# A decoder layer on one core: cross-attention with turned scores, per 512 tokens

## The chip, the cores and the metric

The kernel runs on one core of a Trainium2 chip. Engines: TensorE (PE), VectorE (DVE), ScalarE (ACT), GpSimd (POOL) and SyncE (SP), which only issues DMAs here. The metric is the device time of one execution in microseconds, median of 3 runs.

## The reference

One pre-norm decoder layer on x [2, 1024, 512] and a context ctx [2, 2048, 512], float32:

```
x = x + attn(layernorm(x))          # 16 heads of 32, q and k normed to length 1, band |j-i| <= 16, even distances
x = x + xattn(layernorm(x), ctx)    # one head of 512:
      q = xn @ Wq + bq;  k = ctx @ Wk + bk;  v = ctx @ Wv + bv
      out = softmax(q @ k.T) @ v
x = x + ffn(x)                      # silu(x @ wg.T) * (x @ wu.T) @ wd.T, hidden 1536, int weights / 127
```

Since softmax rows sum to one, the kernel computes cross-attention as softmax(q' ctx^T) ctx Wv + bv with q' = (xn Wq + bq) Wk^T: keys and values are never built.

## The kernel before

The work is a straight list of instructions for each engine; semaphores order them. Nearly all products are float32 in three parts: each operand is split into a high part (rounded to fp32r, by ACT) and a low part (the rest, by DVE), and `three` (line 173) issues high x high, high x low, low x high.

**Self-attention.** Tokens are in NS = 4 sequences of 512. A sequence has 16 slots (`UN`), one head group and token tile each; in a slot PE does scores of the next slot, some work of the neighbouring sequences (norm transposes, projections, output and query projections of the sequence before), and `weighted`. POOL masks the exps, normalises q and k (`scale_units`, ahead of `heads`) and scales outputs. PSUM has 8 banks: `score` (4) and `work` (4). The work banks are a ring: `ring_uses` (line 69) lists every use in order, `take` waits until the use four before is freed. Ahead of the slots come the weights: `part_hi` (ACT) and `part_lo` (DVE) split one part after the other, among them the query and key weights of cross-attention and the output weights (part `WO`, in slot 12 of the first sequence). `turned` splits a normalised, transposed x tile, which the first projections need. `bias_row(("ob",), ...)` makes the output bias from the value bias and the output weights with 12 matmuls, in slot 14 of the first sequence, behind `heads`. Query projections (`project_query`, key "z") give q' in xs and go to DRAM (`qp_scratch`).

**Cross-attention** (`cross_programs`, line 1272) goes over 16 tiles of 128 queries. The turned context `ct_h`/`ct_l` and the context `cn` of one batch lie whole in SBUF in both parts; pieces of 256 context positions come through a staging ring. For a tile g, interleaved with tile g + 1's scores:

- `pe_scores`: 4 banks of [128 queries, 512 context positions], 12 matmuls each with q as the stationary operand
- DVE takes the row maxima from PSUM (`dve_maxima`, `dve_shifts`); ACT computes the exps with row sums (`act_exps`)
- `pe_pt`: 16 transposes turn the exps to [context, queries] (line 1669); ACT and DVE split them (lines 1474, 1549)
- 48 matmuls with 16 context blocks sum [128 queries, 512] in `work[:, 2]`; ACT scales by 1/sum
- `turn`: 4 transposes (line 1679), split, `project`: 12 matmuls with Wv; DVE adds x1 + bv; SP stores x2

Tiles 0 and 1 overlap the end of the last self-attention sequence; the last tile overlaps the transposes of the feed-forward part.

**Feed-forward** (`ffn_programs`): two halves of 1024 tokens, 12 iterations (`NIT`), each with 14 products (a 7-product scheme for gate and up) and, one iteration later, 8 down products. `pe_turn` makes seven turned combinations of the tokens; six of the first half are made during the last cross-attention tile, the seventh in iteration 0. POOL makes token combinations (`pool_tokens`) and weight sums (`pool_weights`).

Of the kernel before, what the change touches and what calls it, by code (L numbers as in the profile page):

```python
# [20 lines left out]
P = 128  # L21
# [31 lines left out]
NSTAGE = 4  # L53
NEARLY = 11
FIRST = 11
# [7 lines left out]
def value_parts(s, n):  # L63

    first = 7 if s == NS - 1 else 4
    return (n - first,) if first <= n < first + ST else ()


def ring_uses():
# [7 lines left out]
    for s in range(NS):  # L77
        more = s + 1 < NS
        for n in range(UN):
            t = n % ST  # L80
            if n == 6:
                yield from (("kt", s, 2), ("qt", s, 2))
# [25 lines left out]
            if not s and n == 14:  # L108
                yield ("ob",)
# [5 lines left out]
    yield from (("o", s, 0), ("o", s, 1), ("o", s, 2), ("y", s, 0), ("o", s, 3), ("y", s, 1), ("pt", 0), ("y", s, 2),  # L115
                ("pt", 1), ("y", s, 3), ("pt", 2))
    yield from (("z", s, m) for m in range(DK))
    yield ("pt", 3)


class Ring:


    def __init__(self, sem, work):
        self.work, self.order = work, list(ring_uses())
        self.nth = {key: n for n, key in enumerate(self.order)}
        self.filled, self.act_freed, self.dve_freed, self.pt_freed = (
            sem(n) for n in ("filled", "act_freed", "dve_freed", "ptl_done"))
        kind = {"v": self.act_freed, "z": self.act_freed, "pt": self.pt_freed}
        self.freed_by = [kind.get(key[0], self.dve_freed) for key in self.order]  # L130
        self.taken = []
# [4 lines left out]
    def wait_filled(self, eng, key):  # L136
        eng.wait_ge(self.filled, sum(k[0] not in ("len", "pt") for k in self.order[:self.nth[key] + 1]))

    def wait_freed(self, eng, key):
        n = self.nth[key]  # L140
        eng.wait_ge(self.freed_by[n], sum(f is self.freed_by[n] for f in self.freed_by[:n + 1]))

# [37 lines left out]
def decoder_layer(nc, x, ctx_n, ctx_t, wqkv_t, qkv_b, wo_t, out_b, wq_t, bq, wk_t, bk, wv, bv,  # L180
# [3 lines left out]
    qp_dram = nc.dram_tensor("qp_scratch", [NT, P, D], F32, kind="Internal").ap()  # L184
    with ExitStack() as ctx:
# [14 lines left out]
        small = [sb(ctx, f"x_{n}", [P, w]) for n, w in (("mx", 4), ("negm", 2), ("shift", 2), ("sums", 4), ("rinv", 2))]  # L200
        at = nc.sbuf_base + -nc.sbuf_base % 32
        links = {n: sem(n) for n in ("exp_done", "pv_done", "o_copied", "x1_stored", "qp_stored", "cb_done")}
        ffn = ffn_programs(nc, Plan(nc, at), sem, score, work, ident, mhalf, wait_pad,
                           wg_t, wu_t, wd_t, x2_dram, out)
        cross = cross_programs(nc, Plan(nc, at), sem, score, work, ident, q_const, small, ring, links,
# [5 lines left out]
def attention_phase(nc, ctx, plan, sem, score, ident, mhalf, wait_pad, q_const, work, ring, links,  # L211
# [158 lines left out]
    qp_v = qp_dram.rearrange("(s t) p n -> s p t n", t=ST)  # L370

    with nc.Block() as block:
        @block.sync
        def _(sp):
# [10 lines left out]
            def store_q(s):  # L385
                wait_freed(sp, ("z", s, DK - 1))
                sp.dma_start(qp_v[s], xs[:]).then_inc(qp_stored, 16)
# [23 lines left out]
            for s in range(NS):  # L411
# [7 lines left out]
                if s == NS - 1:  # L419
# [3 lines left out]
                    cross.load_piece(sp, 0)  # L423
                    cross.load_piece(sp, 1)
                    sp.wait_ge(pv_done, s * UN + UN // 2)
                    cross.load_piece(sp, 2)
                    cross.load_q(sp, 1)
                    for n in range(3, 8):
                        cross.load_piece(sp, n)
# [5 lines left out]
            cross.load_q(sp, 2)  # L435
            for n in range(8, 12):
                cross.load_piece(sp, n)
            store(NS - 1)
            for n in range(12, 16):
                cross.load_piece(sp, n)  # L440
# [121 lines left out]
        def _(act):  # L562
# [81 lines left out]
            def query(s, m):  # L644
                key = ("z", s, m)
                wait_filled(act, key)
                if m == 0:
                    act.wait_ge(x1_stored, 16 * s + 16)
                A.activation(xs[:, :, P * m:P * m + P], bank(key).rearrange("p (t c) -> p t c", t=ST),
                             ACT.Identity, bias=bqp[:, m:m + 1]).then_inc(act_freed, 1)  # L650
# [15 lines left out]
            squares(0, 0, 1)  # L666
# [1831 lines left out]
```

## Time and profile before

| | us |
|---|---|
| median of 3 runs | 1216.77 (1216.16 to 1216.86) |
| profiled execution | 1214.97 |
| its span | 1212.8 |
| PE busy | 1178.3 (97%) |
| DVE / ACT / POOL busy | 746.7 / 494.9 / 418.8 |

Busy times of PE come from modelled ends: matmuls overlap, so the distance of their starts is their cost, not their duration. "Idle before" names who released a waiting engine. The granted clock is in shares of 2.4 GHz.

### The profile page before, as it was taken

To read this page: it belongs to the slowest core of one execution; us is meant where nothing else is said; L and a number is where in the kernel's file an instruction comes from. 1 tells how busy PE (TensorE), PEld (TensorE's weight loads), DVE (VectorE), ACT (ScalarE), POOL (GpSimd) and SP (SyncE) were. 2 spreads that over 40 slices of the span, in tenths; PEclk is the share of its full clock that TensorE was granted. 3 is DMA by queue.
4 is the path that set the end of the run, shared out by engine and by line. 5 is a ranking of instruction groups with operands and counts; after the bars stand their busy time and mean duration, and the time that the engine had idled before them with its cause. 6 is when DMAs were issued, how large, how long until landed. Compare 5 with 4: busy or idle time off the path is not lost.

```text
span 1212.8 us, 17589 instructions
## 1 busy us (share of the span) xinstructions
PE 1178.3 (97%) x6672; PEld 956.6 (79%) x6672; DVE 746.7 (62%) x1268; ACT 494.9 (41%) x854; POOL 418.8 (35%) x382
## 2 busy tenths in 40 slices
PE   6999999999999999999999999999999998999998
PEld 4877777777767888888778888877888887888886
DVE  6667675684686642333563422346899877788875
ACT  5354454454364532222542222236444344444431
POOL 1255765764764010000000100042545742444431
PEclk9999999999999999999999999999999999999999
DMA  8010110201046440000442010021511111511101
GB/s 286 10 36 9 37 62 1 79 36 37 35 140 200 150 154 27 27 26 26 152 127 96 27 35 26 17 79 54 198 53 53 52 53 52 174 53 53 53 18 70
DMA packets 50188, 87.03 MB, mean 72 GB/s; under 512 B 4544, under 2 KB 16832, under 8 KB 50112
## 3 DMA queue, kind: packets, MB, share of 16 engines
q1 hardware_dynamic: 50112, 86.00, 21.5%
q8 instruction: 50, 0.82, 0.3%
q14 instruction: 26, 0.21, 0.1%
HBM read 69.21 MB, written 16.78 MB: 71 GB/s over the span
## 4 chain that ended last, share of the span: by engine, by line
PE 83%; DVE 6%; ACT 4%; POOL 4%; issue 3%; DMA 0%; ACTq 0%; POOLq 0%; DVEq 0%
PE work L175 15%; PE work L177 14%; PE work L176 14%; PE score L177 5%; PE score L175 5%; PE score L176 5%; PE score L2370 4%; PE score L2372 3%; PE score L2371 3%; PE score L1125 2%; PE work L2370 2%; PE work L2372 2%; PE work L2371 2%; PE work L1669 2%; PE score L1139 1%
## 5 line engine op out<-in xcount | busy, mean ns | idle before, releaser
L1549 DVE TENSOR_TENSOR pt_l<-work,pt_h 128x512 fp32r<-128x512 f32 x64 | 44.0, 690 | 168.8 <-ACT pt_h L1474 168.8
L1447 POOL TENSOR_TENSOR xr<-xr,bv_row 128x512 f32<-128x512 f32 x16 | 22.0, 1374 | 333.1 <-DMA xr<-x_scratch 333.1
L2036 POOL TENSOR_TENSOR hid<-fg,hid 128x512 fp32r<-128x512 f32 x48 | 84.8, 1787 | 105.2 <-ACT hid L2100 105.2
L497 POOL TENSOR_TENSOR probs<-probs,band 128x544 f32<-128x544 f32 (+1 forms) x64 | 89.5, 1399 | 78.2 <-ACT probs L628 77.9
L1474 ACT CAST pt_h<-work 128x512 fp32r<-128x512 f32 x64 | 37.3, 587 | 173.1 <-PE work L1669 173.0
L175 PE MATMUL score<-ct_h,x_q_h 128*128 128x512 f32 x256 | 102.8, 401 | 1.6 <-DVE ct_l L1543 1.0
L175 PE MATMUL work<-cn,pt_h 128*128 128x512 f32 x256 | 101.8, 398 | 0.0
L177 PE MATMUL score<-ct_h,x_q_l 128*128 128x512 f32 x256 | 100.1, 391 | 0.0
L177 PE MATMUL work<-cn,pt_l 128*128 128x512 f32 x256 | 99.9, 390 | 0.0
L175 PE MATMUL work<-wqkv_h,xt_h 128*128 128x512 f32 (+1 forms) x256 | 94.9, 371 | 5.2 <-DVE xt_l L804 5.2
L176 PE MATMUL score<-ct_l,x_q_h 128*128 128x512 f32 x256 | 99.9, 390 | 0.0
L176 PE MATMUL work<-cn,pt_h 128*128 128x512 f32 x256 | 99.7, 389 | 0.0
L2248 DVE SCALAR_TENSOR_TENSOR fx<-work,fx 128x512 f32<-128x512 f32 x96 | 65.6, 685 | 40.3 <-PE work L177 40.2
L2370 PE MATMUL score<-fxt,w_hl 128*128 128x512 f32 x222 | 87.1, 392 | 2.2 <-DVE fxt L2196 2.1
L176 PE MATMUL work<-wqkv_l,xt_h 128*128 128x512 f32 (+1 forms) x256 | 88.6, 346 | 0.0
L177 PE MATMUL work<-wqkv_h,xt_l 128*128 128x512 f32 (+1 forms) x256 | 88.1, 344 | 0.0
L2372 PE MATMUL score<-fxt,w_hl 128*128 128x512 f32 x222 | 86.5, 390 | 0.0
L2371 PE MATMUL score<-fxt,w_hl 128*128 128x512 f32 x222 | 86.4, 389 | 0.0
L175 PE MATMUL work<-wd_hl,hid 128*128 128x512 f32 x176 | 68.7, 390 | 0.6 <-DVE fx L2248 0.6
L176 PE MATMUL work<-wd_hl,hid 128*128 128x512 f32 x176 | 68.5, 389 | 0.0
L177 PE MATMUL work<-wd_hl,hid 128*128 128x512 f32 x176 | 68.5, 389 | 0.0
L2100 ACT CAST hid<-fg 128x512 fp32r<-128x512 f32 x48 | 29.7, 621 | 86.8 <-DVE fg L2233 52.0
(243 smaller groups left out, 3025.5 us busy)
## 6 DMA issues: line engine op xcount, KB each, us to landing
x_stage<-in_ctx_t SPq DMA_DIRECT2D x16, 512.0 KB, 4.4
x_stage<-in_ctx_n SPq DMA_DIRECT2D x16, 512.0 KB, 4.8
w_stage<-in_wg_t SPq DMA_DIRECT2D x12, 512.0 KB, 3.7
w_stage<-in_wu_t SPq DMA_DIRECT2D x12, 512.0 KB, 3.7
wd_raw<-in_wd_t SPq DMA_DIRECT2D x12, 512.0 KB, 3.6
x_in<-in_x SPq DMA_DIRECT2D x16, 256.0 KB, 2.7
xs<-in_x SPq DMA_DIRECT2D x4, 1024.0 KB, 5.6
x_scratch<-xs SPq DMA_DIRECT2D x4, 1024.0 KB, 4.4
```

The source lines that it names most:

```text
L175: pe.matmul(out, hi_s, hi_m, start=first, stop=False)
L176: pe.matmul(out, hi_s, lo_m, start=False, stop=False)
L177: return pe.matmul(out, lo_s, hi_m, start=False, stop=last)
L497: PL.tensor_tensor(probs[:, n % 2, :, 0:w], probs[:, n % 2, :, 0:w], band[:, c0:c0 + w].unsqueeze(1).to_broadcast([P, HPG, w]), ALU.mult). ...
L1474: nc.scalar.copy(pt_h[:, 4 * c:4 * c + 4, :], src.rearrange("p (k q) -> p k q", q=P)).then_inc(pth_done, 1)
L1549: V.tensor_tensor(pt_l[:, 4 * c:4 * c + 4, :], src.rearrange("p (k q) -> p k q", q=P), pt_h[:, 4 * c:4 * c + 4, :].bitcast(F32), ALU.subtr ...
L2036: PL.tensor_tensor(hid[:, q, 1, :], g[:, q, :], hid[:, q, 0, :].bitcast(F32), ALU.subtract).then_inc(hidl_done, 1)
L2100: A.copy(hid[:, q, 0, :], g[:, q, :]).then_inc(hidh_done, 1)
L2248: V.scalar_tensor_tensor(xs[:, t, :], work[:, 2 + n % 2, :], WSCALE, xs[:, t, :], ALU.mult, ALU.add)\
L2370: PE.matmul(bank(key), w_h, x_h, start=first, stop=False, skip_group_check=True)
L2371: PE.matmul(bank(key), w_h, x_l, start=False, stop=False, skip_group_check=True)
L2372: last = PE.matmul(bank(key), w_l, x_h, start=False, stop=k == 1, skip_group_check=True)
```

## The change

Cross-attention is written anew, the feed-forward part gets other SBUF places and another start, and the first sequence is reordered.

**Scores turned.** The stationary operand is a block of 128 context positions, the moving one 512 queries of a sequence. j counts 64 slots = 4 sequences x 16 context blocks; a slot is one block of scores (12 matmuls, 18 slots ahead, `LEAD`) and one block of the context product (12 matmuls into 4 banks, result [512 channels in 4 blocks, 512 queries]):

```
+    def pe_scores(pe, j):
...
+            last = three(PE, out, ct_h[:, n % 2, k, c], ct_l[:, n % 2, k, c], q_h[g % 2][:, k, :], q_l[g % 2][:, k, :],
                          k == 0, k == DK - 1)
+    def pe_weighted(pe, j):
...
+            last = three(PE, score[:, d, :], cn_h[:, m % 2, j % 2, c], cn_l[:, m % 2, j % 2, c],
+                         pt_h[:, j % 2, :], pt_l[:, j % 2, :], i == 0, i == CK - 1)
     def pe_program(pe):
+        for j in range(NSL):
+            if j + LEAD < NSL:
+                pe_scores(pe, j + LEAD)
+            if j and not i:
+                pe_sums(pe, g - 1)
+            if i == CK - 2 and g + 1 < NS:
+                pe_maxima(pe, g + 1)
+            if i == CK - 1 and g + 1 < NS:
+                pe_shift(pe, g + 1)
+            if j in RESULT_AT:
+                pe_project(pe, RESULT_AT[j])
+            pe_weighted(pe, j)
```

`pe_pt`, `turn` and the copy scaled by 1/sum are gone. Scores are now copied by ACT to a ring of 20 blocks in SBUF:

```
+    def act_scores(act, j):
+        A.copy(s_at(j), s_bank(j)).then_inc(sc_copied, 1)
+    def dve_maxima(dve, j):
+            V.tensor_tensor(mx[:], mx[:], s_at(j), ALU.max).then_inc(mx_done, 1)
+    def dve_sub(dve, j):
+        V.tensor_tensor(s_at(j), s_at(j), shifts[j // CK % 2][:], ALU.add).then_inc(sub_done, 1)
+    def act_probs(act, j):
...
+        A.activation(pr[:, j % 2, :], s_at(j), ACT.Exp).then_inc(e_done, 1)
+        act.wait_ge(e_done, j + 1)
+        if j >= 2:
+            act.wait_ge(block_done, j - 1)
+        A.copy(pt_h[:, j % 2, :], pr[:, j % 2, :]).then_inc(pth_done, 1)
+    def dve_probs(dve, j):
+        V.tensor_tensor(pt_l[:, j % 2, :], pr[:, j % 2, :], pt_h[:, j % 2, :].bitcast(F32), ALU.subtract)
+    def pool_sum(pool, j):
+            nc.gpsimd.tensor_tensor(acc[:], acc[:], pr[:, j % 2, :], ALU.add).then_inc(acc_done, 1)
```

Once a sequence: `pe_maxima` transposes the running maxima (4), `dve_shift` reduces them, forms the shift per query and copies it wide (`spread`), `pe_shift` multiplies it by the identity (4 float32 matmuls of 128 columns) so that it stands along the free dimension, `act_shift` copies it; `pe_sums` sums the running sum over partitions (4 matmuls of one column). At a sequence's end `act_out`/`dve_out` split the four banks and `pe_project` (12 matmuls, four times, in slots 1 to 4 of the next sequence) multiplies by Wv; 1/sum is applied in `dve_result`. Context and turned context are no longer kept: each piece of 256 positions is loaded and split again for every sequence, two buffers each (ct in even slots, cn mostly in odd ones, in slots 46 to 60 in even ones). The order on ACT and DVE in a slot is: piece, exp and cast (ACT) or add and low part (DVE) for slot j + 1, then copy or maximum of block j + 18.

**Hand-overs.** Blocks 0 to 3 of the scores stand in slots 12 to 15 of the last self-attention sequence, 4 to 17 behind it between the output and query projections:

```
+    yield from (("c", 4), ("c", 5), ("c", 6), ("o", s, 0), ("o", s, 1), ("c", 7), ("o", s, 2), ("y", s, 0), ("c", 8),
+                ("o", s, 3), ("y", s, 1), ("c", 9), ("y", s, 2), ("c", 10), ("c", 11), ("y", s, 3))
+    yield from (("c", j) for j in range(12, CK))
+    yield from (("z", s, 0), ("mt",), ("z", s, 1), ("mb",), ("z", s, 2), ("z", s, 3))
+    yield from (("c", j) for j in range(CK, LEAD))
```

Feed-forward statistics, norms, weight parts and token combinations are spread over slots 28 to 50; five turned combinations stand in slots 52, 54, 57, 60 and 61, two in iteration 0, together with the last sequence's four projections and results.

**First sequence.** ACT, and likewise DVE: turned tiles ahead of weight parts, the query weights' part last:

```
             part_hi(0)
+            turned("x", 0, 0, xt_h, x_hi)
             part_hi(1)
-            turned("x", 0, 0, xt_h, x_hi)
             part_hi(2)
+            turned("x", 0, 1, xt_h, x_hi)
             part_hi(3)
             norm1(0, 2)
-            turned("x", 0, 1, xt_h, x_hi)
             norm1(0, 3)
+            turned("x", 0, 2, xt_h, x_hi)
             part_hi(KEYS)
+            squares(0, 0, 0)
+            turned("x", 0, 3, xt_h, x_hi)
+            squares(0, 0, 1)
             part_hi(WQ)
-            squares(0, 0, 0)
-            turned("x", 0, 2, xt_h, x_hi)
-            squares(0, 0, 1)
-            turned("x", 0, 3, xt_h, x_hi)
```

The output weights are split in slot 3 (ACT) and 4 (DVE) instead of 12, and the bias row moves ahead of `heads` in slot 6:

```
                     if n == 6:
+                        if not s:
+                            pe.wait_ge(set_lo, WO + 1)
+                            bias_row(("ob",), 1, wo_h, wo_l)
                         heads(s, 2)
...
-                    if not s and n == 14:
-                        pe.wait_ge(set_lo, WO + 1)
-                        bias_row(("ob",), 1, wo_h, wo_l)
```

## Rows read from the trace of the kernel before

**Rows 1.** Page, busy time and chain: engine, us, share, instructions; shares of the span

```profile
PE 1178.3 (97%) x6672; PEld 956.6 (79%) x6672; DVE 746.7 (62%) x1268; ACT 494.9 (41%) x854; POOL 418.8 (35%) x382
...
PE 83%; DVE 6%; ACT 4%; POOL 4%; issue 3%; DMA 0%; ACTq 0%; POOLq 0%; DVEq 0%
```

**Rows 2.** Busy time in stretches: PE, weight loads, DVE, ACT, POOL, granted clock, DMA

```profile
0.00:26.00 26.00, 14.11 (x53) 10.86 (x54) 15.79 (x35) 12.78 (x17) 5.57 (x24) 1.00 0.92 323
350.00:400.00 50.00, 47.81 (x284) 36.84 (x282) 36.84 (x61) 24.88 (x42) 23.65 (x23) 0.97 0.49 162
400.00:840.00 440.00, 436.88 (x2103) 361.73 (x2102) 180.05 (x325) 148.41 (x286) 42.84 (x34) 1.00 0.21 67
```

**Rows 3.** Order of time on PE in cross-attention: start us, us, what

```profile
543.39 0.60 PE L1679 MATMUL work<-ident,x_o 128*128 128x128 f32 x4
...
563.18 0.39 PE L175 MATMUL work<-cn,pt_h 128*128 128x512 f32 x1
...
566.58 0.60 PE L1669 MATMUL work<-ident,x_pr 128*128 128x128 f32 x4
566.94 0.48 PE L175 MATMUL score<-ct_h,x_q_h 128*128 128x512 f32 x1
...
570.21 0.60 PE L1679 MATMUL work<-ident,x_o 128*128 128x128 f32 x4
```

**Rows 4.** Groups of instructions of PE: busy us, mean ns, idle before

```profile
L1669 PE MATMUL work<-ident,x_pr 128*128 128x128 f32 x256 | 38.1, 272 | 1.3 <-DVE pt_l L1549 1.3
L1094 PE MATMUL work<-cols,wk_raw 128*128 128x1 f32 x32 | 3.7, 251 | 0.0
```

**Rows 5.** Waits of PE, 838 to 860: us in total, times, longest

```profile
PE work L2370 <- DVE xr L1579: 0.8, 1, 0.8
```

**Rows 6.** Groups of instructions of ACT, DVE and POOL

```profile
L637 ACT COPY o_sc<-score 128x512 f32<-128x512 f32 x16 | 9.6, 597 | 0.0
L1482 ACT ACTIVATE x_pr<-score,x_shift 128x512 f32<-128x512 f32 x64 | 43.1, 687 | 36.4 <-DVE x_shift L1564 36.4
L1474 ACT CAST pt_h<-work 128x512 fp32r<-128x512 f32 x64 | 37.3, 587 | 173.1 <-PE work L1669 173.0
L1468 ACT CAST cn<-x_stage 128x1024 fp32r<-128x1024 f32 x16 | 15.9, 1056 | 0.0
L1549 DVE TENSOR_TENSOR pt_l<-work,pt_h 128x512 fp32r<-128x512 f32 x64 | 44.0, 690 | 168.8 <-ACT pt_h L1474 168.8
L1543 DVE TENSOR_TENSOR cn<-x_stage,cn 128x1024 fp32r<-128x1024 f32 x16 | 20.2, 1288 | 3.1 <-ACT cn L1468 3.0
L2008 POOL TENSOR_TENSOR tn<-fxn 128x1024 f32<-128x1024 f32 x2 | 4.8, 2396 | 5.8 <-DVE fxn L2184 5.8
```

**Rows 7.** Durations: minimum, median, maximum in ns, first and last start

```profile
L2191 DVE TENSOR_TENSOR w_hl<-wsum,w_hl x24: 1208/1225/2316, 820.9 to 1171.9; 128x1024 fp32r<-128x1024 f32 x24
L1447 POOL TENSOR_TENSOR xr<-xr,bv_row x16: 1281/1292/2333, 426.0 to 799.7; 128x512 f32<-128x512 f32 x16
```

**Rows 8.** Order of time at the start: start us, us, what, idle before

```profile
10.76 0.79 PE L175 MATMUL work<-wqkv_h,xt_h 128*128 128x512 f32 x1 [2.07 <-DVE xt_l L804]
20.46 0.47 PE L175 MATMUL work<-wqkv_h,xt_h 128*128 128x512 f32 x1 [0.83 <-DVE xt_l L804]
25.72 0.66 PE L175 MATMUL work<-wqkv_h,xt_h 128*128 128x512 f32 x1 [2.28 <-DVE xt_l L804]
27.02 0.63 PE L175 MATMUL work<-wqkv_h,xt_h 128*128 128x512 f32 x1
16.69 1.91 ACT L568 CAST wq_h<-wq_raw 128x2048 fp32r<-128x2048 f32 x1
20.23 2.28 DVE L815 TENSOR_TENSOR wq_l<-wq_raw,wq_h 128x2048 fp32r<-128x2048 f32 x1
```

**Rows 9.** Order of time in the first sequence, slots 3 and 6

```profile
75.38 0.80 ACT L579 ACTIVATE xn<-x_in,nb,rstd 128x512 f32<-128x512 f32 x1
83.35 1.09 PE L1078 MATMUL work<-ident,qk 128*128 128x128 f32 x8 [0.96 <-POOL qk L491]
```

More of the change, by code:

```diff
@@ L422, in _ @@
                     wait_filled(sp, ("qt", s, 3))
[L423 to L429, printed above, removed]
+                    for n in range(5):
+                        cross.load_ct(sp, n)
                 if s:
@@ L1461, in act_query @@
-    def act_query(act, g, par):
-        act.wait_ge(q_landed, g * 16 + 16)
-        nc.scalar.copy(q_h[:, par, :], q_raw[:]).then_inc(q_hi, 1)
-    def act_split(act, n):
-        act.wait_ge(staged[slot(n)], 16 * sum(slot(m) == slot(n) for m in range(n + 1)))
-        src, hi, _ = split_views(n)
-        nc.scalar.copy(hi, src).then_inc(split_hi, 1)
-    def act_pt(act, g, c):
-        act.wait_ge(pt_ready, g * 4 + c + 1)
-        src = ring.bank(("pt", c)) if starts(g) else work[:, c % 2, :]
-        nc.scalar.copy(pt_h[:, 4 * c:4 * c + 4, :], src.rearrange("p (k q) -> p k q", q=P)).then_inc(pth_done, 1)
@@ L1476, in act_exps @@
-    def act_exps(act, g, par):
-        act.wait_ge(shift_done, g + 1)
-        if not starts(g):
-            act.wait_ge(pt_ready, g * 4)
-            act.wait_ge(sum_done, g)
-        for c in range(SB):
-            nc.scalar.activation(pr[:, 512 * c:512 * c + 512], score[:, c, :], ACT.Exp,
-                                 bias=shift[:, par:par + 1], accum_out=sums[:, c:c + 1]).then_inc(e_done, 1)
-    def act_finish(act, g):
-        act.wait_ge(tr_ready, g + 1)
-        nc.scalar.copy(ot_h[:], work[:, 3, :]).then_inc(oth_done, 1)
@@ new lines, in pe_shift, with pe_sums @@
+    def pe_shift(pe, g):
+        out = ring.take(pe, ("mb",)) if not g else work[:, 3, :]
+        pe.wait_ge(spread_done, g + 1)
+        for t in range(ST):
+            last = PE.matmul(out[:, P * t:P * t + P], spread[:, t, :], ident[:], start=True, stop=True)
+        last.then_inc(mb_ready, 1)
+    def pe_sums(pe, g):
+        pe.wait_ge(acc_done, (CK - 1) * (g + 1))
+        if not g:
+            pe.wait_ge(one_done, 1)
+        if g + 1 < NS:
+            pe.wait_ge(mb_copied, g + 2)
+        else:
+            pe.wait_ge(rinv_done, g)
+        for t in range(ST):
+            last = PE.matmul(work[:, 3, t:t + 1], acc[:, P * t:P * t + P], one[:], start=True, stop=True)
+        last.then_inc(rs_ready, 1)
@@ new lines, in pe_project @@
+    def pe_project(pe, n):
+        g, t = n // ST, n % ST
+        pe.wait_ge(otl_done, DK * g + DK)
+        if not n:
+            pe.wait_ge(wv_lo, 2)
+            ring.wait_last(pe, 2)
+        elif n <= (NS - 1) * ST:
+            pe.wait_ge(x2_done, n)
+        elif t == 1:
+            pe.wait_ge(rinv_done, NS)
+        else:
+            pe.wait_ge(x2_done, n - 1)
+        c = slice(P * t, P * t + P)
+        for d in range(DK):
+            last = three(PE, y_bank(n), ot_h[:, d, c], ot_l[:, d, c], wv_h[:, d, :], wv_l[:, d, :],
+                         d == 0, d == DK - 1)
+        last.then_inc(y_ready, 1)
@@ L1881, in ffn_programs @@
     uses = [key for key in events if key[0] == "x" or (key[0] == "p" and key[3] != 2)]
-    nth_use = {key: n for n, key in enumerate(uses)}
-    banks = [score[:, i, :] for i in range(4)] + [work[:, i, :] for i in range(2)]
+    banks = [work[:, i, :] for i in range(2)] + [score[:, i, :] for i in range(4)]
+    bank_of, last_in, use_ahead, n_ring = {}, {}, {}, 0
+    for key in uses:
+        if key[0] == "x" and key[1] == 0 and key[2] < NPROD - 1:
+            i = key[3] + (0 if key[2] < NTURN else 4)
+        else:
+            i, n_ring = n_ring % len(banks), n_ring + 1
+        bank_of[key], use_ahead[key], last_in[i] = i, last_in.get(i), key
+    first_in = {i: next(key for key in uses if bank_of[key] == i) for i in range(2, len(banks))}
     W_AT = (0, 2, 1, 3, 4, 5, 6)
```

1306 lines of the change are left out of this document (705 added, 601 removed).

## The prediction

> **What bounds the kernel now.** I read the page's busy table and chain first. TensorE (PE) is busy 97% of the span and holds 83% of the chain that ended last; VectorE (DVE) has 6% of the chain, ScalarE (ACT) and GpSimd (POOL) 4% each [rows 1]. So the time is PE's instruction stream plus the places where it stands still. The busy time by stretch shows where it does: 11.9 us in the first 26, 2.2 us in 350 to 400 (hand-over to cross-attention), 3.1 us in the 440 us of cross-attention [rows 2]; the feed-forward part the change hardly touches. In cross-attention the reader is to see a stream without holes, in which DVE is busy 41% of the time, ACT 34% and POOL 10%. There, only an instruction taken from PE is worth its price; other engines' work is free as long as it fits under PE's.
>
> **The change, part by part.** Sums are against the profiled execution, 1214.97 us (2.2 us around a span of 1212.8); the median of the runs is 1.8 us above it.
>
> *1. Transposes removed.* With a tile of 128 queries as the moving result's rows, exp(scores) had to be turned before the context product: 16 transposes a tile, and 4 more for the context vector before the value weights. With the scores computed as [context position, query], neither exists. What they cost on PE: 512-column matmuls start 3.40 us apart for 15, 0.227 us each, and there is no wait in the stretch [rows 3]. A tile has 48 of them for scores, 48 for context, 12 for the value projection: 108 x 0.227 = 24.55 us. The tiles follow at 26.82 us (543.39 to 570.21) [rows 3]. The remaining 2.27 us are its 20 transposes. A group of four starts 0.36 us before the next matmul [rows 3]; five such groups are 1.8 us, and the matmuls behind a group start late too. I take the period: 16 tiles x 2.27 = -36.3 us. The lower bound from the bare group, 80 x 0.36, is -28.8 us. The matmuls themselves keep their number: scores 64 pieces x 12, context 64 x 12, projection 16 x 12, all of 512 columns, as before.
>
> *2. Small PE work added.* Per 512 queries (four times): four transposes of the maxima, four 128-column products that spread the shift over all partitions, four one-column products that sum the exps. Transposes: 4 x 0.454 = 1.8 us. One-column: 32 took 3.7 us [rows 4], 0.116 each, 1.9 us for 16. The float32 product of 128 columns is in no row. Below it stands a transpose (0.09), above it a 512-column matmul (0.227); I take 0.17, 2.7 us for 16, nearer neither. Sum +6.3 us (5.1 to 7.4). The Trainium skill ("FP8 and Floating Point Precision") gives true float32 four passes of the array; by it an estimate is 512 columns' worth, the upper end, 0.9 us more.
>
> *3. Old hand-over stalls removed.* 2.2 and 3.1 us [rows 2] and the 0.8 us for the last result at the border of the feed-forward part [rows 5]: waits for context pieces, the normalised tile, the exps and the result of a tile at each border. The score products of pieces 0 to 3 now lie in slots 12 to 15 of the last sequence, so the chain store, reload of xs, bias, norm starts one 2.73 us block earlier against PE, and the wait for the first turned tile goes: -6.1 us.
>
> *4. New work of the other engines, in a slot of 24 matmuls = 5.46 us.* ACT: copy of the scores 0.60, exp 0.69, cast 0.59, one cast of a 1024-column piece 1.06: 2.9 us. DVE: add shift, maximum, low part at 0.69 each, low part of the piece 1.29: 3.4 us. POOL: one running sum 1.29 us [rows 6]. All under 5.46, so 46 of 64 slots cost nothing. Queries (two casts of 1024), results and first feed-forward pieces add 1 to 2.5 us in single slots; scores run 18 pieces ahead and exps one slot, which absorbs a slot that is long once. If this cover were gone, each 0.1 us over a slot would cost 4.6 us in all. SP: each slot issues at most one 512 KB load of either kind, landing in 4 to 5 us, two slots ahead of its cast; the stores of results and reloads of x1 stand in the same queue, but a result's slot is 8.2 us long.
>
> *5. The last 18 slots.* No scores are left, so a slot is 12 matmuls, 2.73 us. At the last border the maxima, their turning, the shift and its spreading follow each other with only 2.73 us blocks beside them. DVE needs the reduction and the spread copy at 0.69 each (512 columns, as its low part [rows 6]) and three small ones, 0.2 each by my estimate, against a block already half used by probabilities and a context piece: 1.2 us late. Then copy 0.6, add 0.69, exp 0.69, cast 0.59, low part 0.69 against 3.2 us of PE; behind them four context banks must be cast and freed at 0.6 to 0.7 each, and slot 49's add waits behind these on DVE: about 0.3 + 1.0 + 1.5. That is 4 us. Slots with a context piece (8) have ACT 1.06 + 0.69 + 0.59 and DVE 0.69 as one chain, 3.0 against 2.73, about 0.3 each: 2 us. Then the shared resource. DVE's 1024-column low part takes 1.208 us at least and 2.316 at most, and POOL's xr add 1.281 to 2.333 [rows 7]: now and then one of them stands for about the other's whole duration. In slots 46 to 52 four token combinations of POOL (2.40 each [rows 6]) come on top of the sums: I give this 2 us. Sum +8 us (2 to 15). The rule in the Trainium skill ("SBUF — State Buffer", "Who interferes with whom") says it outright: an operation of DVE with two SBUF inputs and one of POOL that reads SBUF lock each other out for the whole instruction; the maxima and medians of [rows 7] agree. This speaks against the change, which moves work from PSUM operands to SBUF ones and gives POOL a sum in every slot.
>
> *6. Start of cross-attention and entry of the feed-forward part.* Before, the wait for a late piece covered part of the last group's chain (reciprocals, POOL scale, low part) beside the three score blocks; now the output projection arrives first and waits 0.8 us. Two turned pieces and four projections move into the first feed-forward iteration, where no down products stand yet, so DVE has room: 1 us for bank waits (0 to 3). Sum +1.8 us.
>
> *7. First sequence.* PE waits 2.07 us for the first low part, 0.83 for the third tile's, 2.28 for the fourth's [rows 8]. The turned tile went on DVE behind two weight parts (of 0.87 us) and goes behind one: 0.9 us. The third and fourth stood behind the query weights' cast and low part (1.91 and 2.28 us [rows 8]), which now follow: 3.1 us. After the fourth wait matmuls start 0.43 us apart, 0.227 later: the 1.2 GHz level of two, behind those two waits [rows 8]; without them 1.7 us may go. Against it stands a new wait of 0.3 to 0.6 us for the query weights before their bias row, and the key weights' low part on DVE comes only 1.1 us earlier, so heads may wait. I take -4.5 us of 5.4 (0 to -6).
>
> *8. Output bias row in slot 6.* Twelve matmuls move, none goes. In slot 6 they lie ahead of heads, which waited 0.96 us for POOL's scaling [rows 9], and 0.3 for a bank. But the 128x2048 cast (1.91 us) now stands in slot 3 ahead of a norm that starts at 75.38 [rows 9] and whose transposes run at 76.75: 1.3 to 1.6 us of wait in slot 4. DVE's low part leaves slot 12 and lets its reciprocal go sooner, POOL's scale for the next heads stays hidden. Net 0 (-2 to +2).
>
> Sum: -36.3 + 6.3 - 6.1 + 8 + 1.8 - 4.5 + 0 = -30.8 us: 1184.2 for the profiled execution, 1186 for the median.
>
> **The rivals.** *A, the lock makes the tail DVE- and POOL-bound.* Serial work on two-input SBUF operations in slots 46 to 52: DVE 7 x 1.2 + 4 x 1.14 + 2.1 = 15.1 us, POOL 7 x 1.29 + 9.6 + 4 x 1.29 = 23.8 us, together 38.9 against PE's 31.7, and nearly even afterwards. Then item 5 is 18 to 22 us rather than 8, and single slots with queries or feed-forward pieces give another 3: 1198 to 1202. For it: the maxima of [rows 7]. Against: DVE and POOL overlap most of the time in the feed-forward part. *B, the start gives nothing:* the bias row and heads simply wait where the tiles did, because DVE's key-weight chain is only 1.1 us earlier, and slot 4's wait remains: 1186 + 4.5 + 1.5 = 1192. *C, a slot is bound by its own chain*: copy, maximum, piece's cast and low part, add, exp, cast, low part one behind the other make 0.60 + 0.69 + 1.06 + 1.29 + 0.69 + 0.69 + 0.59 + 0.69 = 6.3 us in 5.46. If the buffers (two of exps, two of pieces) didn't let them overlap, 64 x 0.84 = 54 us: 1240, slower. It turns at 0.47 us over a slot (30.6/64). Against: each stage has a second buffer and its own engine; the old tiles ran as long a chain (transpose, cast, low part) with 1.3 us idle before 256 transposes [rows 4]. *D, fewer stalls than I count:* tail 2, start -6, entry 0: 1177.
>
> **Numbers.** Forecast with its small variations 0.58, A 0.17, B 0.13, C 0.04, D 0.08. The range holds forecast, B, D and most of A: 1176 to 1203. A change of 0.2% (2.4 us) is about what a measurement of this kernel tells from none. Faster 0.95, same 0.01, slower 0.04 (C).
>
> **What would show it.** Right: no transposes of probabilities or context vectors; PE's 512-column count unchanged; in cross-attention up to the last border PE at 100% in nearly every stretch, slots at 5.46 us; waits of PE gathered at the last border and the 18 slots behind it, on DVE's low parts of the probabilities or context banks; first slot of attention some 4 us earlier. Wrong: PE waiting for probabilities in ordinary slots (C), DVE's two-input operations at twice their length throughout the tail (A), an unchanged end of the first projections (B), a spreading product far above 0.23 us.

## The result, and the profile after

The changed kernel takes 1222.7 us (median; the kernel before, timed beside it, 1216.8): ratio 1.0059, 95% interval 1.0043 to 1.0076. The forecast of 1186 and its range are missed, with the wrong sign. The profiled execution has a span of 1221.0 us, 8.2 more than before. Of the executions of the runs below, two (1467 and 1640 us) are slow ones, with a lower granted clock; medians and ratios are of the others.

The busy line of the page, after (engine, us, share, instructions):

```profile
PE 1162.9 (95%) x6432; PEld 941.3 (77%) x6432; DVE 862.7 (71%) x1292; ACT 551.7 (45%) x866; POOL 519.3 (43%) x443
```

Against [rows 1] PE is busy 15 us less and idle 24 us more; DVE is busy 116 us more, POOL 100. Where PE stands is in the stretches (columns as in [rows 2]):

```profile
350.00:400.00 50.00, 48.37 (x260) 37.83 (x257) 26.41 (x33) 18.29 (x29) 19.66 (x18) 0.92 0.41 138
400.00:722.00 322.00, 321.76 (x1454) 266.73 (x1454) 230.58 (x292) 162.34 (x236) 94.27 (x67) 1.00 0.37 124
722.00:820.00 98.00, 78.73 (x329) 62.73 (x328) 66.69 (x74) 40.57 (x64) 42.97 (x26) 0.90 0.21 65
820.00:860.00 40.00, 32.86 (x137) 26.53 (x136) 13.62 (x22) 13.33 (x21) 8.36 (x11) 0.87 0.24 77
```

Up to 722, the slots with scores, PE idles 0.2 us in 322. Then come 98 us for the last 18 slots, in which it idles 19.3 us and has 0.90 of its clock (another 9.8 us), and 40 us at the entry of the feed-forward part with 7.1 us idle at 0.87 (5.2 us). (The two kinds of loss overlap by 1 to 2 us, where PE waits at the lower clock.) The waits of PE in 722 to 820, and in 820 to 870 (what waits, for whom; us in total, times, longest):

```profile
PE score L190 <- DVE pt_l L1691: 8.8, 6, 2.2
PE work L1806 <- DVE x_spread L1683: 5.8, 1, 5.8
PE work L190 <- DVE xr L1709: 4.5, 1, 4.5
...
PE score L2530 <- ACT m L2256: 5.0, 1, 5.0
PE work L190 <- DVE xr L1709: 2.1, 1, 2.1
```

Time spent beyond the matmuls' and transposes' own pace (0.227 us per 512 columns, 0.09 per transpose), by stretches that begin and end at the same work in each profile. The losses hold to some 1.5 us, since they hang on the pace taken for the small operations:

| stretch | before | after |
|---|---|---|
| last product of self-attention ends at, less the score blocks now inside it | 368.0 | 370.0 |
| from there to the first feed-forward product | 462.9 | 449.1 |
| of it: up to the last border (maxima turned, 380.9 to 721.7) | | 340.8, nothing lost |
| of it: last border and 18 slots (721.7 to 819.1) | | 97.4, 30.3 lost |
| first feed-forward product to first down product | 30.3, 1.9 lost | 50.3, 12.5 lost (9.4 of work moved in) |
| from there to the end | 348.0 | 348.0 |

Three places, then: the last 18 slots, the entry of the feed-forward part, the hand-over to cross-attention. The traces suggest a cause in each, and the experiments try them.

**The hand-over.** In 350 to 400 the granted clock is 0.92, before it was 0.97 [rows 2]. PE waits 4.0 us at 347.6 for the normalised tile xn and 1.6 us at 352.1 for a turned tile, and runs at 1.2 GHz for 10.2 us from 347.9 on; before, it waited 1.7 us for xn and ran at 1.2 GHz for 3.4 us. On ACT, after, the casts of the first query block stand ahead of that norm:

```profile
344.74 1.99 ACT L1548 CAST x_q_h<-x_q_raw 128x1024 fp32r<-128x1024 f32 x2
346.63 0.81 ACT L598 ACTIVATE xn<-xs,nb,rstd 128x512 f32<-128x512 f32 x1
```

**The last border.** Order of time on DVE and on POOL, after (start us, us, what):

```profile
726.64 1.58 DVE L1678 SCALAR_TENSOR_TENSOR x_negm<-x_mx,q_const 128x4 f32<-128x4 f32 x1
728.26 0.16 DVE L1680 TENSOR_TENSOR x_shift<-x_negm,q_const 128x4 f32<-128x4 f32 x1
728.45 2.45 DVE L1683 COPY x_spread<-x_shift 128x512 f32<-128x512 f32 x1
```

```profile
725.42 2.79 POOL L2170 TENSOR_TENSOR tn<-fxn 128x1024 f32<-128x1024 f32 x1
728.28 2.34 POOL L2173 TENSOR_TENSOR tn<-fxn,tn 128x1024 f32<-128x1024 f32 x1
```

An operation on four columns takes 1.58 us and the spread copy 2.45, and neither ends before POOL's token combination beside it: the combinations end at 728.2 and 730.6, the two operations at 728.2 and 730.9. The four-column operation that starts between the two combinations takes 0.16. PE waits 5.8 us for the copy.

**A bare slot.** DVE and ACT, after, around 800:

```profile
799.88 0.68 DVE L1687 TENSOR_TENSOR x_s<-x_s,x_shifts 128x512 f32<-128x512 f32 x1
801.91 1.24 DVE L1691 TENSOR_TENSOR pt_l<-x_pr,pt_h 128x512 fp32r<-128x512 f32 x1 [1.35 <-ACT pt_h L1583]
803.07 0.68 DVE L1687 TENSOR_TENSOR x_s<-x_s,x_shifts 128x512 f32<-128x512 f32 x1
```

```profile
800.59 0.63 ACT L1579 ACTIVATE x_pr<-x_s 128x512 f32<-128x512 f32 x1 [2.12 <-DVE x_s L1687]
801.26 0.62 ACT L1583 CAST pt_h<-x_pr 128x512 fp32r<-128x512 f32 x1
```

Add, exp, cast, low part, and the next slot's add only behind that low part: 3.19 us round, against 2.73 of matmuls. Behind a turned tile it is worse, since ACT's exp and DVE's add stand behind copies that wait for PE's transposes. One such slot, on ACT, DVE and PE:

```profile
771.40 1.07 ACT L2249 CAST fxt<-work 128x512 fp32r<-128x512 f32 x2 [3.59 <-PE work L2513]
773.22 0.68 DVE L1687 TENSOR_TENSOR x_s<-x_s,x_shifts 128x512 f32<-128x512 f32 x1
773.94 0.63 ACT L1579 ACTIVATE x_pr<-x_s 128x512 f32<-128x512 f32 x1 [1.46 <-DVE x_s L1687]
775.25 1.21 DVE L1691 TENSOR_TENSOR pt_l<-x_pr,pt_h 128x512 fp32r<-128x512 f32 x1 [1.35 <-ACT pt_h L1583]
776.61 0.47 PE L190 MATMUL score<-pt_h,cn_h 128*128 128x512 f32 x1 [2.08 <-DVE pt_l L1691]
```

**The entry.** POOL, ACT and the DMA queue of SP, after:

```profile
835.04 1.29 POOL L1514 TENSOR_TENSOR xr<-xr,bv_row 128x512 f32<-128x512 f32 x1 [16.48 <-DMA xr<-x_scratch]
844.10 1.29 POOL L1514 TENSOR_TENSOR xr<-xr,bv_row 128x512 f32<-128x512 f32 x1 [7.77 <-DMA xr<-x_scratch]
845.36 0.74 POOL L2193 TENSOR_TENSOR wsum<-w_stage 128x256 f32<-128x256 f32 x1
```

```profile
848.33 1.05 ACT L2242 CAST w_hl<-wsum 128x1024 fp32r<-128x1024 f32 x1 [14.86 <-POOL wsum L2201]
853.39 0.57 ACT L2256 COPY m<-score 128x512 f32<-128x512 f32 x1
```

```profile
838.92 0.32 SPq L1446 DMA_DIRECT2D x_scratch<-xr  x1
841.32 0.32 SPq L1442 DMA_DIRECT2D xr<-x_scratch  x1
```

Result tile 13 is computed, stored (838.92), tile 15's residual loaded into its place (841.32), POOL adds the bias (844.10), and only then makes the weight sums that stand behind it in its order; ACT waits 14.9 us for these with the copy of m, which frees a bank, behind, and PE waits 5.0 us for that copy. Before, all but the last tile's projection ran ahead of the feed-forward part, and PE's one wait for a result at this border was 0.8 us [rows 5].

### The profile page after: what moved, and what is told of

It is laid out like the page before. It is cut to its first block, busy times and chain, and to the rows that moved or that the text cites. A ratio compares the mean times of both kernels' runs of the same rounds, so it can differ in the third digit from the quotient of the medians.

```text
span 1221.0 us, 17222 instructions
## 1 busy us (share of the span) xinstructions
PE 1162.9 (95%) x6432; PEld 941.3 (77%) x6432; DVE 862.7 (71%) x1292; ACT 551.7 (45%) x866; POOL 519.3 (43%) x443
## 4 chain that ended last, share of the span: by engine, by line
PE 78%; DVE 10%; ACT 4%; POOL 4%; issue 3%; DMA 1%; SPq 0%; ACTq 0%; DVEq 0%; POOLq 0%
PE work L190 15%; PE work L192 14%; PE work L191 14%; PE score L190 4%; PE score L192 4%; PE score L191 4%; PE score L2530 4%; PE score L2532 4%; PE score L2531 4%; PE score L1157 2%; PE work L2530 2%; PE work L2532 2%; PE work L2531 2%; PE score L1171 1%; DVE fxt L2357 1%
## 5 line engine op out<-in xcount | busy, mean ns | idle before, releaser
L1510 POOL TENSOR_TENSOR x_acc<-x_acc,x_pr 128x512 f32<-128x512 f32 x56 | 84.2, 1503 | 190.5 <-ACT x_pr L1579 190.5
L190 PE MATMUL score<-pt_h,cn_h 128*128 128x512 f32 x256 | 103.8, 406 | 9.0 <-DVE pt_l L1691 8.8
L1691 DVE TENSOR_TENSOR pt_l<-x_pr,pt_h 128x512 fp32r<-128x512 f32 x64 | 82.4, 1287 | 41.8 <-ACT pt_h L1583 41.8
L192 PE MATMUL score<-pt_h,cn_l 128*128 128x512 f32 x256 | 101.7, 397 | 0.0
L191 PE MATMUL score<-pt_l,cn_h 128*128 128x512 f32 x256 | 101.6, 397 | 0.0
L190 PE MATMUL work<-x_q_h,ct_h 128*128 128x512 f32 x256 | 100.4, 392 | 0.0
L191 PE MATMUL work<-x_q_l,ct_h 128*128 128x512 f32 x256 | 99.8, 390 | 0.0
L192 PE MATMUL work<-x_q_h,ct_l 128*128 128x512 f32 x256 | 99.7, 389 | 0.0
L190 PE MATMUL work<-wd_h,hid 128*128 128x512 f32 x176 | 68.7, 390 | 0.6 <-DVE fx L2409 0.6
L192 PE MATMUL work<-wd_h,hid 128*128 128x512 f32 x176 | 68.5, 389 | 0.0
L191 PE MATMUL work<-wd_l,hid 128*128 128x512 f32 x176 | 68.5, 389 | 0.0
```

Of the source, the lines that this page charges most:

```text
L190: pe.matmul(out, hi_s, hi_m, start=first, stop=False)
L191: pe.matmul(out, hi_s, lo_m, start=False, stop=False)
L192: return pe.matmul(out, lo_s, hi_m, start=False, stop=last)
L1510: nc.gpsimd.tensor_tensor(acc[:], acc[:], pr[:, j % 2, :], ALU.add).then_inc(acc_done, 1)
L1691: V.tensor_tensor(pt_l[:, j % 2, :], pr[:, j % 2, :], pt_h[:, j % 2, :].bitcast(F32), ALU.subtract)\
```

## The experiments

All are the changed kernel with the edit shown, unless said otherwise. Ratios are to the kernel before, timed on the same chip; the changed kernel's is 1.0059 (1.0043 to 1.0076). The kernel before took 1216.8 us beside the changed one, 1215.2 beside the first four runs, 1216.1 beside the next three and the new start alone, 1215.4 beside the up weights later and the bias row alone; so a difference of a microsecond or two between medians is to be read from the ratios.

| run | median us | ratio, interval | span | last 18 slots | entry |
|---|---|---|---|---|---|
| query casts behind the norm | 1220.3 | 1.0040 (1.0024 to 1.0056) | 1218.1 | 98.1 | 49.9 |
| four residual tiles | 1216.5 | 0.9995 (0.9983 to 1.0008) | 1216.0 | 97.4 | 42.9 |
| add one slot ahead | 1218.1 | 1.0019 (1.0008 to 1.0030) | 1214.0 | 90.7 | 50.2 |
| no running sum | 1217.6 | 1.0002 (0.9986 to 1.0019) | 1215.9 | 90.2 | 50.2 |
| three orders in the tail | 1208.2 | 0.9933 (0.9916 to 0.9950) | 1209.1 | 82.9 | 49.9 |
| GpSimd's order | 1222.7 | 1.0050 (1.0034 to 1.0067) | 1222.6 | 96.6 | 49.8 |
| all mends | 1194.8 | 0.9827 (0.9813 to 0.9841) | 1193.1 | 79.7 | 39.0 |
| all, up weights later | 1193.3 | 0.9826 (0.9806 to 0.9846) | 1191.6 | 79.6 | 38.9 |
| before, new start alone | 1215.5 | 0.9992 (0.9981 to 1.0002) | 1212.3 | | |
| before, bias row alone | 1216.7 | 1.0008 (0.9997 to 1.0019) | 1217.6 | | |

### Query casts behind the norm

```diff
-  slot 10, ACT: act_query(0, 0); act_query(0, 1); ... norm2(s - 1, 3)
+  slot 10, ACT: ... norm2(s - 1, 3); act_query(0, 0)     slot 11: act_query(0, 1)
-  slot 10, DVE: dve_query(0, 0); dve_query(0, 1)
+  slot 10, DVE: dve_query(0, 0)                          slot 11: dve_query(0, 1)
```

> The changed kernel with one edit: in the last sequence the casts of the first query block go one half behind the norm of slot 10 and one half in slot 11 on ACT, and one half each in slots 10 and 11 on DVE (there both stand in slot 10, ahead of the norm's output for the last query tile). Theory 'order': the hand-over's waits of 3.97 us (at 347.6) and 1.63 us (at 352.1) and 5.1 us of the 10.2 us at half clock behind them go: 8 to 10 us less than the changed kernel's 1222.7, so 1213 to 1215. Rival 'the same work later': the casts then come late for the first score block in slot 12 and the PE waits there instead; under 3 us less, 1220 to 1223.

The theory missed on size, the rival on cause. From the first product of probabilities and values to the last one of self-attention it takes 319.0 us in place of 321.8; the whole is shorter by 2.9 us in the span and 2.3 by the ratios, whose intervals overlap. That is within the rival's range, but nothing waits for the casts in slot 12. The wait for xn fell from 4.0 to 2.4 us, not to nothing, and the time at 1.2 GHz behind it from 10.2 to 6.8 us. What is left isn't the casts: ACT's norm at 344.68 waits 0.2 us for POOL's nb, and before it ACT waits for POOL's o_sc. In the changed kernel slot 10 has no value projection (they stand in slots 7, 8, 8, 9), so PE arrives earlier than the chain allows. That reading is argued from the trace, not tried.

### Four residual tiles

```diff
+    xr += [put("xr2", 125440, [P, D]), put("xr3", 154112, [P, D])]   # x_shifts0, x_spread
...
-                for n in range(2):
+                for n in range(ST):
                     load_xr(sp, (NS - 1) * ST + n)
...
```

> The changed kernel with one edit: the last two of the 16 result tiles get tiles of their own for the residual (over the space of x_shifts0 and x_spread, which are free by then) in place of the two that first have to be stored, so their loads start in slot 60 and GpSimd adds bv_row to them by about 821. Theory 'store, load, add, weight sums': GpSimd's wsum starts at about 827 in place of 845, ACT doesn't wait 14.9 us for it, and the PE's 5.0 us wait at 854 and the 3.4 us that the half clock costs behind it go: 7 to 9 us less than 1222.7, so 1214 to 1216. Rival 'ACT is late anyway' (table load, turned tiles, three silus in front of the copy of m): 2 us or less, 1220 to 1223.

The theory holds: entry 50.3 to 42.9 us, 1222.7 to 1216.5 (7.8 us by the ratios). POOL adds all four in one go and makes the sums 7.3 us after the entry, in place of 26 (order of time on POOL):

```profile
817.97 5.49 POOL L1520 TENSOR_TENSOR xr<-xr,bv_row 128x512 f32<-128x512 f32 x4
828.84 0.74 POOL L2199 TENSOR_TENSOR wsum<-w_stage 128x256 f32<-128x256 f32 x1 [5.37 <-ACT w_stage L2235]
```

The wait of 5.0 us for m is 0.6; the one of 2.1 us for the result stays, as it should, since this edit doesn't touch it.

### Add one slot ahead

```diff
-            if i < CK - 1:
+            if i < CK - 1 and j <= NSL - CK:
                 dve_sub(dve, j + 1)
+            if NSL - CK <= j < NSL - 2:
+                dve_sub(dve, j + 2)
```

> The changed kernel with one edit: from slot 48 on DVE adds the shift to the scores one slot earlier, ahead of the low part of the probabilities. Theory 'chain in series': a bare slot of the last 16 takes 3.19 us on the chain add 0.68, exp 0.63, cast 0.62, low part 1.21, because DVE's next add stands behind that low part, against 2.73 us of matmuls; with the add ahead only the DVE's own 1.9 us is left, and ACT's exp no longer waits for the DVE behind a turned tile. The waits of 2.08, 2.06 and 2.20 us at 774, 784 and 797 and the small ones go, with 3 us of half clock: 7 to 10 us less than 1222.7, so 1213 to 1216. Rival 'lock': GpSimd's running sum holds the low part at 1.21 us and the order does nothing: 0 to 2 us, 1221 to 1223.

The order counts: 97.4 to 90.7 us in the last 18 slots; the waits for the low part go from 8.8 to 5.7 us. The gain is 7.0 us in the span and 4.6 in the median, at the lower end of what the theory said or under it; the lock (an operation of DVE and one of POOL that hold each other up) takes a part back. With the add freed from its place it runs at the same time as POOL's sum, and its mean goes from 0.8 to 1.4 us (groups of DVE in 745 to 816, after and this run; us, mean ns):

```profile
L1687 DVE TENSOR_TENSOR x_s<-x_s,x_shifts 128x512 f32<-128x512 f32 x10 | 8.2, 820 | 0.0
```

```profile
L1687 DVE TENSOR_TENSOR x_s<-x_s,x_shifts 128x512 f32<-128x512 f32 x9 | 12.2, 1357 | 0.0
```

### No running sum

```diff
         else:
-            nc.gpsimd.tensor_tensor(acc[:], acc[:], pr[:, j % 2, :], ALU.add)
+            nc.gpsimd.tensor_tensor(acc[:, 0:1], acc[:, 0:1], pr[:, j % 2, 0:1], ALU.add)   # last 512 queries
```

> The changed kernel, which leaves out GpSimd's running sum of the probabilities for the last 512 queries from its second addition on (one column is still added, so every wait stays). Theory 'lock': the low part of the probabilities takes 0.69 us in place of 1.21 us, a bare slot's chain is 2.65 us and so under the 2.73 us of matmuls; the waits of 2.1 us behind a turned tile shrink to 1.6 us: 3 to 5 us less than 1222.7, so 1218 to 1220, less than the order of the add brings. Rival 'GpSimd's sum is beside the path': the low part stays over 1.1 us or no wait shrinks, 1222 to 1223.

The lock counts too, as the expectation says. Low parts: minimum, median, maximum in ns, first of before (all 64), then of after (all 64), then of this run from 745 on:

```profile
L1549 DVE TENSOR_TENSOR pt_l<-work,pt_h x64: 675/692/693, 399.7 to 815.4; 128x512 fp32r<-128x512 f32 x64
```

```profile
L1691 DVE TENSOR_TENSOR pt_l<-x_pr,pt_h x64: 691/1398/1733, 441.3 to 815.0; 128x512 fp32r<-128x512 f32 x64
```

```profile
L1694 DVE TENSOR_TENSOR pt_l<-x_pr,pt_h x15: 691/693/1619, 744.4 to 809.8; 128x512 fp32r<-128x512 f32 x15
```

With its first input in PSUM the low part never took over 693 ns, also in the 6 of 64 that ran beside an operation of POOL; with both in SBUF and a POOL sum released by the exp ahead of it, it runs beside POOL in 59 of 64 and takes twice that in the median. Without the sum it is 693 again, the last 18 slots are 90.2 us, and the waits behind a turned tile fall from 2.1 to 1.5 us, as expected. Leaving out the sum gives back 7.2 of the 30.3 us lost. Not all of it is the low part's lock: the wait for the result of slot 50, whose residual POOL adds behind its sum, falls by 1.2 us too.

### Three orders in the tail

```diff
   # last 16 slots, on ACT and DVE, with the add one slot ahead
-  act_cn, act_probs(j + 1), act_turned(TURN_AT[j])
+  act_probs(j + 1), act_cn, act_turned(TURN_AT[j - 1])
-  dve_cn, dve_probs(j + 1), dve_turned(TURN_AT[j])
+  dve_probs(j + 1), dve_cn, dve_turned(TURN_AT[j - 1])
```

> The changed kernel with the add one slot ahead (as the run before with that edit alone) and two more orders in the last 16 slots: context halves are cast behind the probabilities of the slot, not ahead of them, and the copies of a turned tile stand one slot later on ACT and DVE, behind the next slot's exponential. With the add ahead alone, 5.7 us of waits for the low part of the probabilities were left (2.2, 1.13, 1.14, 0.4 ...), each in the slot behind a turned tile or a context half. Theory 'in series behind the turned tile': they go to under 1 us, with the half clock at 795: the kernel lies 4 to 6 us under the 1218.1 of the add alone, 1212 to 1214. Rival 'lock': the low part and the add stand in one another's way with GpSimd's sum and 3 us or more of the waits stay: 1216 to 1218.

1208.2: better than either forecast. From 745 to 808, where its feed-forward part begins, PE has one wait left:

```profile
PE work L190 <- DVE xr L1713: 3.6, 1, 3.6
```

All 8.8 us for low parts are gone, with POOL's sums and the lock still there: from 745 on the low parts take 1.0 us in the mean in place of 1.3, but the adds 1.3 in place of 0.8 and POOL's sums 1.6 in place of 1.4. So the lock was not the cause by itself: it lengthened a chain that its order had laid in series. Taken out of series, the longer operations fit beside PE's work. How much each of the three orders brings was tried for the add alone (6.7 of the 14.5 us).

### GpSimd's order

```diff
-            if NSL - LEAD <= j < NSL - LEAD + 4:
-                ffn.pool_tokens(pool, j - NSL + LEAD)
+            if j in TOKENS_AT:      # {48: 0, 53: 1, 56: 2, 58: 3}
+                ffn.pool_tokens(pool, TOKENS_AT[j])
+   # and, in every slot, pool_residual ahead of pool_sum
```

> The changed kernel with two edits on GpSimd alone: the four token combinations of 2.3 to 2.9 us each stand in slots 48, 53, 56 and 58 in place of 46 to 49, and the residual add of a slot ahead of its running sum. Theory 'GpSimd's combinations hold DVE's shift and the first result': the PE's wait for x_spread falls from 5.8 to 3 us or less and the wait for the result of slot 50 from 4.5 us to under 1 us, with 3 to 5 us of half clock behind the two: 8 to 12 us less than 1222.3, 1210 to 1214. Rival 'DVE is full there anyway' (context halves, gate weights, low parts of four tiles): one of the waits stays over 4 us, 1217 to 1222.

A miss for the sum, 1222.7 us, though the first half of the theory holds to the letter. With no combination beside it, the border's chain on DVE reads:

```profile
729.41 0.16 DVE L1679 SCALAR_TENSOR_TENSOR x_negm<-x_mx,q_const 128x4 f32<-128x4 f32 x1
...
729.80 0.43 DVE L1684 COPY x_spread<-x_shift 128x512 f32<-128x512 f32 x1
```

1.58 us has become 0.16 and 2.45 has become 0.43; PE waits 2.4 us for the copy, not 5.8. But the waits moved on (722 to 820):

```profile
PE score L190 <- DVE pt_l L1692: 12.1, 8, 2.4
PE work L190 <- DVE xr L1710: 4.2, 1, 4.2
PE work L1807 <- DVE x_spread L1684: 2.4, 1, 2.4
PE score L190 <- DVE x_ot_l L1697: 2.1, 1, 2.1
```

2.1 us is new for x_ot_l, which stands behind the up weights' pieces on DVE. A combination in slot 48 holds the piece ahead of the add here too (2.40 us for 256 columns, 2.42 in the changed kernel, 0.41 when alone), and the add itself takes 1.77 us in place of 0.68; the result stands on DVE behind the low part that follows from them and is 4.2 us late, as the rival had it (one of the waits over 4 us). Low parts, still in series, are waited for 12.1 us in place of 8.8; that the combinations in slots 53 to 58 are to blame for that is read from the trace. In this kernel the combinations' ten microseconds cost about the same in either place.

### All mends together

```diff
   # the edits above but for the running sum, which stays whole, and in the first feed-forward iteration, DVE:
+            if it == 0:
+                results[1]()
             dve_u4(dve, it, 0)
-            if it == 0:
-                results[1]()
```

> The changed kernel with all edits at once: casts of the first query block behind the norm; tiles of their own for the last two residuals; add ahead, context halves behind the probabilities and turned tiles one slot later in the last 16 slots; GpSimd's order; and one more, the second result ahead of the sums of product 4 on DVE in the first feed-forward iteration (wait of 2.1 us at 839). If each wait found in the trace is a cost by itself the gains add: 1.2 + 5.8 + 8 to 10 + 8 to 12 + 2 to 4 under 1222.3, so 1190 to 1198, under both kernels. Rival 'the waits share a cause or give way to one another': not more than the two largest together, 1203 or more.

The gains add, nearly: 1194.8 us, ratio 0.9827, 28 us under the changed kernel and 21 under the kernel before. In the trace -17.7 us are in the last 18 slots, -11.4 at the entry, -2.5 between the first product of probabilities and values and the end of self-attention; that first product itself comes 3.6 us later in this profile, of which more below. What POOL's new order does here no run separates: against the run with three orders the wait for the spread copy falls from 5.8 to 2.4 us and that for the result from 3.6 to 1.2, low parts are waited for again (3.2 us) and x_ot_l 2.1 us in place of 0.7, and the last 18 slots are 79.7 us in place of 82.9.

> The run with all edits, with one more: the three pieces of the up weights (ACT 0.6, 1.04 and 0.4 us, DVE 0.68, 1.22 and 0.4 us alone) are cast in slots 51, 52 and 54 in place of 46, 47 and 48, where they stand ahead of the first low parts of the context. Theory 'in order behind the pieces': the PE's wait of 2.1 us for x_ot_l at 732 and of 1.2 us for the result at 746 go, with up to 3 us of half clock from 735 on: 3 to 6 us under 1194.8, 1189 to 1192. Rival: the pieces wait for GpSimd in the later slots as well and put the waits for the low part of the probabilities (3.2 us in all) up by as much: 1193 to 1196.

```diff
-            if NSL - LEAD <= j < NSL - LEAD + 3:        # slots 46, 47, 48
+            if j in UP_AT:                              # {51: 0, 52: 1, 54: 2}
                 ffn.act_weights(act, 1, UP_AT[j])       # and the same on DVE
```

The rival was right. The wait for x_ot_l fell from 2.1 to 0.7 us, that for the result rose from 1.2 to 2.2, that for low parts from 3.2 to 3.9, and the last 18 slots take 79.7 and 79.6 us; the ratio is the same. Of the 79.6 some 13 us are still lost.

### The two side edits, each on the kernel before

> The kernel before, with the first sequence's new order on ACT and DVE alone (turned tiles' parts ahead of query weights' parts). Theory: it is worth what the traces of the two kernels showed up to the first scores, 2.5 us: 1212.3 to 1213.3 against 1215.2 for the kernel before on this chip. My prediction had 4.5 us. Rival: the new waits for the query weights' low part (1.4 us) and for qk (1.5 us) give it back by slot 4: 1214.7 to 1215.7.

> The kernel before, with the output bias row's product alone moved from slot 14 to slot 6 of the first sequence (and its weights' parts from slot 12 to slots 3 and 4). Theory (my prediction's step 8): twelve matmuls leave one place and come back in another, 0 us, within 2 us either way: 1214 to 1218 with 1216.1 for the kernel before. Rival: in slot 14 there was a wait and a stretch at half clock at 118 (1.7 us), which go, and the new place costs none: 2 to 3 us less, 1213 to 1214.

(First: the new order of `turned` and the weights' parts on ACT and DVE, as in the change. Second: bias row, its parts and its addition moved as in the change.) The start gives 0.6 us by the medians, between 2.3 less and 0.2 more by the interval; the bias row nothing that can be measured. A single profile would have misled here: the first product of probabilities and values starts at 61.6 us in the profile of before and at 59.1 after, but in ten profiles with the new start it lies between 58.7 and 63.2, and with the old start at 61.6 and 65.6. The traces show what goes with it: from 52 to 57 us on PE runs at 1.2 GHz for a while, 3.4 us in the new-start profiles at 58.7 to 59.1, 6.8 us in those at 61.6 to 62.0, 10.2 us in those at 62.6 to 63.2 (old start: 3.4 us at 61.6, 10.2 at 65.6), while the first scores ahead of it lie within 48.5 and 50.2. Why that stretch is longer in one execution than in another is not shown.

## Why the prediction was wrong, step by step

*Steps 1 to 3, transposes gone, small work added, old stalls gone:* right in sum. The stretch from self-attention to the feed-forward part took 462.9 us; less 9.4 moved on, less 36.3, plus 6.3, less the old 3.1 is 420.4. It took 449.1 with 30.3 lost in the tail, 418.8 without. Spreading took 0.8 us for four products, 0.2 each, beside the 0.17 assumed. That is under the 0.227 that the forecast had estimated from the four passes of the Trainium skill ("FP8 and Floating Point Precision", "TensorE Precision Notes"). The one-column products had been misread: the 32 instructions of [rows 4] are 16 products, for the trace shows two for each float32 product, so 16 cost 3.2 us (0.81 for four at 535.8) and not 1.9.

*Step 4, slots with scores are free:* right. PE idled 0.2 us in 322; the buffers that rival C doubted do overlap there, although the low parts take 1.3 us on the mean and not 0.69.

*Step 5, the last 18 slots, +8 us (2 to 15):* this step failed; 30.3 us were lost. It had the border at 4 us, a context piece at 0.3 a slot, the lock at 2. Measured: 5.8 us of wait for the spread alone, 4.5 for the result of slot 50, 8.8 for low parts, and 9.8 through the clock. What was missing were three things; their gains overlap and can't be added. First, DVE's order: the forecast laid add, exp, cast and low part of one slot in a chain, and called it short of a slot, but never asked what stands behind the low part on DVE. It is the next slot's add, so the chain goes round at 3.19 us. Second, the turned tiles, which put PE's transposes into that round. The run with three orders shows 14.5 us for these two. Third, the lock (7.2 us by the run without sums) was priced as a count of its chances and not where it falls: low part and sum follow the same exp, so they met in 59 of 64 slots, and a four-column operation on the path can be held as long as a combination (1.58 us, and 3.4 of the 5.8 us that PE waits for the spread, by the run with GpSimd's order). The rule that the forecast cited from the Trainium skill ("SBUF — State Buffer", "Who interferes with whom") agrees with the rows above on operations with two inputs in SBUF. The forecast had applied it to these alone; the spread copy has one input and was held too (2.45 us, 0.43 without a combination beside it).

*Rival A (1198 to 1202)* came nearest to the tail, with 18 to 22 us from serial sums of two engines' work. Its cause holds for part of the border's wait; for the low parts the runs don't bear it out: with all sums and locks in place their waits went to nothing by order alone. *Rival C* (slot bound by its own chain) had been turned down for all 64 slots; a chain of its kind, without copy and maximum, is what binds in the 18 in which a slot is half as long. I had set its price for a slot of 5.46 us only.

*Step 6, start of cross-attention and entry, +1.8 us:* failed. The entry lost 10.6 us more than before, of which the run with four tiles gives back 7.4; with all mends, the earlier result on DVE among them, the rest is gone too (39.0 us). I had costed the four projections as matmuls and bank waits, and not followed what their results release: store, load, an addition on POOL, and the weight sums that stand behind it there. At the hand-over the casts of the queries ahead of a norm cost 2.8 us; by these two profiles the whole stands 6 us worse than forecast. The other 3 stand in what the run with later casts leaves, waits of 2.4 and 1.6 us and 6.8 us at 1.2 GHz (3.4 before), and no run takes these away.

*Step 7, first sequence, -4.5 us:* about -1 (-2.3 to +0.2). Of the old waits for turned tiles the first fell from 2.1 to 1.4 us and the others did go, but wq_l (1.4 us) and qk (1.5 us) took their place: rival B's mechanism. *Step 8, bias row, 0:* right.

In sum the span's 39.0 us between forecast (-30.8) and trace (+8.2) are 22.3 in the tail, 9.6 at the entry, and 7.1 left over, at start and hand-over. The mends brought back 28 of them.

**A stall costs twice.** In the tail and at the entry PE waits seven times for 2 us or more, and at six of these waits, in them or within 1.5 us behind, its granted clock fell from 2.4 to 1.2 GHz for 3.4 or 6.8 us: 0.90 over the tail, 0.87 over the entry, against 1.00 in the 322 us before. That was about 15 of the 43 us lost in those two stretches, and the forecast had no term for it there.

## What to carry to other kernels

When blocks of the bounding engine get shorter (here 5.46 to 2.73 us, when the scores ran out), draw the round of each helper engine again: from one instruction to the same one a slot later, through everything that stands before it in order, not only the latency of one slot's chain. When work is moved across a border, follow what its result releases, through stores, loads and in-order queues, to the last engine. And price two operations that exclude each other where they meet, not by how often they might; one that is harmless beside slack is dear on a four-column operation that everyone waits for.

## What was not expected of the hardware

An operation of DVE on 128x4 elements took 1.58 us beside a POOL operation of 2.79 and 0.16 without it, a 128x512 copy 2.45 and 0.43, a 128x256 difference 2.42 and 0.41: the small one lasts to about the large one's end. And in profiles of kernels with the same start the first product of probabilities and values stands up to 4.5 us apart, with stretches of 3.4 to 10.2 us at 1.2 GHz ahead of it, so that one profile can't tell an edit there.
